# Skipping the padding rows of indirect transfers in a graph-attention and mixture-of-experts kernel

## What is computed

```python
def reference(x, src, dst, ...):
    x = x + gnn(layernorm(x), edge_index, W1, a_src1, a_dst1, b1, W2, a_src2, a_dst2, b2)
    x = x + ffn(layernorm(x), Wg, bg, We, be, W1, b1, W2, b2)

def ffn(xf, ...):                       # G=4 groups, E=8 experts each, D=768, M=384
    ggates, gidx = topk_gates(xf @ Wg + bg, 2)
    egates, eidx = topk_gates(einsum('nd,gde->nge', xf, We) + be, 4)
    combine = gw[:, :, None] * ew
    for g in range(G):
        h = gelu(einsum('nd,edm->enm', xf, W1[g]) + b1[g][:, None, :])
        o = einsum('enm,emd->end', h, W2[g]) + b2[g][:, None, :]
        y = y + einsum('end,ne->nd', o, combine[:, g, :])
```

## Time and profile before

| | |
|---|---|
| median of the runs | 1545.75 us (1545.67 to 1548.69) |
| span of the profiled execution | 1547.4 us |
| PE busy | 1367.3 us, 88% of the span |
| DVE busy | 1158.1 us, 75% |
| ACT busy | 741.6 us, 48% |
| POOL busy | 493.7 us, 32% |
| bytes moved by DMA | 222.06 MB, of them 78.63 MB on the queue that GpSimd issues |
| mixing and routing | about 657 to 816 us of the span |
| expert stage | about 816 us to the end |

### The profile page before, as it was taken

The page is one execution under the profiler, slowest core; times in us unless marked ns, Lnnn a source line. Parts: engine busy times, 40 slices in busy tenths (PEclk is TensorE's granted clock), DMA queues, the critical chain, the costliest instruction groups (busy, mean ns, idle before and its releaser), DMA issues. The chain is left out here.

```text
span 1547.4 us, 30224 instructions
## 1 busy us (share of the span) xinstructions
PE 1367.3 (88%) x7686; PEld 1137.4 (74%) x7687; DVE 1158.1 (75%) x1817; ACT 741.6 (48%) x1175; POOL 493.7 (32%) x554
## 2 busy tenths in 40 slices
PE   6888988878778879799957999999999999999995
PEld 3656656733223339799956899999999999989895
DVE  5479999899999978858886566555565656787782
ACT  3465565255555553412214455444454545665662
POOL 1000000003333410032324445545555545454563
PEclk9999999799999989999977999999999999999998
DMA  4300002041222223144577888877788887999974
GB/s 168 136 10 17 17 14 74 17 176 60 72 93 72 68 59 128 57 124 114 124 206 249 212 231 223 185 182 170 178 210 202 211 203 181 238 282 283 248 163 83
DMA packets 101759, 222.06 MB, mean 144 GB/s; under 512 B 16551, under 2 KB 55719, under 8 KB 101586
## 3 DMA queue, kind: packets, MB, share of 16 engines
q1 hardware_dynamic: 78690, 140.50, 28.3%
q0 software_dynamic: 22240, 78.63, 24.9%
q10 hardware_dynamic: 784, 2.36, 0.4%
HBM read 161.78 MB, written 55.74 MB: 141 GB/s over the span
## 5 line engine op out<-in xcount | busy, mean ns | idle before, releaser
L972 PE MATMUL ps_o<-prob,h_head 128*97 128x512 f32 (+1 forms) x480 | 188.4, 530 | 51.2 <-DVE prob L914 51.2
L2022 POOL DMA_INDIRECT out_nodes<-y,to_index x92 | 153.4, 1667 | 217.4 <-DMA out_nodes<-y,to_index 194.1
L2307 PE MATMUL ps_h<-e_hi,e_xt_hi 128*128 (+1 forms) x546 | 195.7, 359 | 10.4 <-ACT e_xt_hi L2126 6.0
L2292 PE MATMUL ps_y<-e_hi,e_ht_hi 128*128 (+1 forms) x546 | 191.0, 350 | 9.7 <-issue 7.1
L972 PEld LDWEIGHTS ps_o<-prob,h_head 128*97 128x97 f32 x480 | 73.5, 165 | 165.5 <-issue 90.2
L2307 PE MATMUL ps_h<-e_lo,e_xt_hi 128*128 (+1 forms) x546 | 187.3, 343 | 0.0
L2292 PE MATMUL ps_y<-e_hi,e_ht_lo 128*128 (+1 forms) x546 | 183.7, 336 | 0.0
L2292 PE MATMUL ps_y<-e_lo,e_ht_hi 128*128 (+1 forms) x546 | 183.6, 336 | 0.0
L2190 DVE TENSOR_TENSOR e_lo<-raw,e_hi (+1 forms) x189 | 175.6, 953 | 6.2 <-ACT e_hi L2134 5.9
L2143 ACT ACTIVATE y<-ps_y,gate 128x768 f32 (+1 forms) x91 | 82.2, 904 | 170.1 <-PE ps_y L2292 160.4
L2011 POOL DMA_INDIRECT landing<-table,index x93 | 131.3, 1412 | 82.7 <-DVE in_rows L2242 48.1
(11 more groups left out here) (333 smaller groups left out, 3066.0 us busy)
## 6 DMA issues: line engine op xcount, KB each, us to landing
raw<-in_ew SPq DMA_DIRECT2D x192, 384.0 KB
w_room<-rel_dram SPq DMA_DIRECT2D x14, 640.0 KB, 4.7
b_all<-in_eb SPq DMA_DIRECT2D x32, 192.0 KB
al_src<-al_dram SPq DMA_DIRECT2D x1, 5000.0 KB, 14.7
xs<-in_x SPq DMA_DIRECT2D x5, 768.0 KB, 12.8
x_in_t<-in_x SPq DMA_DIRECT2D x10, 384.0 KB, 3.6
out_nodes<-x SPq DMA_DIRECT2D x10, 384.0 KB, 4.1
table<-xf SPq DMA_DIRECT2D x10, 384.0 KB, 2.6
```

The lines of the kernel that those rows point to most:

```text
L972: turn = nc.tensor.matmul(ps_o[u][0:C1 + 1, c, 0:WID[c]], h_head[:, u, t, :], prob[:, t % 2, 512 * c:512 * c + WID[c]], start=(t == 0), st ...
L2022: nc.gpsimd.indirect_dma_start(out, bass.IndirectOffsetOnAxis(to_index[:, w:w + 1], 0), y[:, w, :], None, bounds_check=ROWS - 1, compute_o ...
L2292: last = nc.tensor.matmul(ps_y[:, half, 0:HALF], a, b[:, bass.ds(u, 1), at:at + HALF].rearrange("p o d -> p (o d)"), start=(m == 0), stop= ...
L2307: nc.tensor.matmul(ps_h[:, 0:HID], xt_hi[:, c, :], b[:, bass.ds(e % 2, 1), c * HID:(c + 1) * HID] .rearrange("p o m -> p (o m)"), start=(c ...
```

## The change

Padding keeps its numbers `NP + lane`, but the indirect transfers now have their bound at `NP - 1` and `oob_is_err=False`, so that rows with a larger index are skipped. The 128 extra rows of the table and of the output go, with the two stores that set them to zero and the waits for these. A skipped row of a gather leaves in the landing buffer what was there; so both landing buffers are set to zero once, by two ScalarE copies of a zero tile (the former `pad_rows`, still set by GpSimd) between the last mixing matmul and the first weights, and the first gather waits for these.

```diff
-ROWS = NP + P
...
-        pad_rows = sb("pad_rows", [P, TW])
+        zero_rows = sb("zero_rows", [P, TW])
...
-                sp.wait_ge(filled, 3)
-                sp.dma_start(s.table.ap()[NP:ROWS, :], pad_rows[:, :]).then_inc(pad_out, 16)
-                sp.dma_start(out[NP:ROWS, :], pad_rows[:, 0:D]).then_inc(pad_out, 16)
...
-                sp.wait_ge(pad_out, 32)
...
                     nc.gpsimd.indirect_dma_start(out, bass.IndirectOffsetOnAxis(node_i[:, t:t + 1], 0),
-                                                 bias[:, t % 2, :], None, bounds_check=ROWS - 1,
+                                                 bias[:, t % 2, :], None, bounds_check=NP - 1, oob_is_err=False,
                                                  compute_op=ALU.add).then_inc(added, 16)
...
-                pool.wait_ge(pad_out, 32)
+                pool.wait_ge(landing_set, 2)
                 pool.wait_ge(index_set, 1)
                 nc.gpsimd.indirect_dma_start(s.landing[:, 0, :], None, s.table.ap(),
                                              bass.IndirectOffsetOnAxis(s.index[:, 0:1], 0),
-                                             bounds_check=ROWS - 1).then_inc(s.gathered, 16)
+                                             bounds_check=NP - 1, oob_is_err=False).then_inc(s.gathered, 16)
...
                 act.wait_ge(mixed, NT)
+                act.wait_ge(filled, 3)
+                for u in range(2):
+                    nc.scalar.activation(s.landing[:, u, :], zero_rows[:, :], ACT.Copy).then_inc(landing_set, 1)
                 for piece in range(3):
...
                                                  bass.IndirectOffsetOnAxis(index[:, 0:1], 0),
-                                                 bounds_check=ROWS - 1).then_inc(gathered, 16)
+                                                 bounds_check=NP - 1, oob_is_err=False).then_inc(gathered, 16)
...
                                                  bass.IndirectOffsetOnAxis(to_index[:, w:w + 1], 0),
-                                                 y[:, w, :], None, bounds_check=ROWS - 1,
+                                                 y[:, w, :], None, bounds_check=NP - 1, oob_is_err=False,
                                                  compute_op=ALU.add).then_inc(scattered, 16)
...
-        s.table = nc.dram_tensor("table", [ROWS, TW], F32)
+        s.table = nc.dram_tensor("table", [NP, TW], F32)
...
-    out = nc.dram_tensor("out_nodes", (ROWS, D), F32, kind="ExternalOutput")
+    out = nc.dram_tensor("out_nodes", (NP, D), F32, kind="ExternalOutput")
```

More of the change, by code:

```diff
@@ L1396, in mix_and_route @@
         xf_out = [sem("q_xf_out0"), sem("q_xf_out1")]
-        gates_out, pad_out = sem("q_gates_out"), sem("q_pad_out")
+        gates_out, landing_set = sem("q_gates_out"), sem("q_landing_set")
         consts, filled, casts = sem("f_consts"), sem("q_filled"), sem("f_casts")
@@ L1461, in _ @@
                 nc.gpsimd.memset(br[:, E + G:LOGITS], NOT_A_NEIGHBOUR).then_inc(filled, 1)
-                nc.gpsimd.memset(pad_rows[:, :], 0.0).then_inc(filled, 1)
+                nc.gpsimd.memset(zero_rows[:, :], 0.0).then_inc(filled, 1)
                 nc.gpsimd.memset(half_neg[:, :], -0.5).then_inc(consts, 1)
@@ L2028, in add_bias @@
                     nc.gpsimd.indirect_dma_start(out, bass.IndirectOffsetOnAxis(s.node_i[:, t:t + 1], 0),
-                                                 s.bias[:, t % 2, :], None, bounds_check=ROWS - 1,
+                                                 s.bias[:, t % 2, :], None, bounds_check=NP - 1, oob_is_err=False,
                                                  compute_op=ALU.add).then_inc(added, 16)
```

## The result

| | median of 6 runs, us | profiled execution: span, us |
|---|---|---|
| kernel before | 1546.8 (1545.67 to 1548.77) | 1547.4 |
| changed kernel | 1536.03 (1534.71 to 1542.56) | 1533.0 |

The ratio is 0.992, with a 95% interval of 0.990 to 0.994. The forecast was 1543.8 us with a range from 1537.5, so the gain of 10.8 us lies beyond the range, by 1.5 us at its low end.

A forecast was written before the change was run, and what follows sets the result against it. TensorE was taken as the bound in most of the expert stage, with gains only in its gaps. Terms -1.3 (a) and -0.7 (b), the rest 0, gave -2.0 us: 1545.75 to 1543.75, put at 1543.8, range 1537.5 to 1552.

The forecast's parts named there:

- (b): Skipped rows in each expert's last tile: shorter scatter landings, little reaching TensorE; gain 0.7 us, between 0 and 3.8.
- (a): The all-padding scatter of `k = 0` at the expert stage's start: skipping it gains 1.3 us, between 0 and 1.9.
- my sign of 19.5: Sign for (a): PE busy about 19.5 us or more in the 24 us from the empty `k = 0` scatter on.
- (c): GpSimd's indirect-transfer instructions: cost 0, scatter's median and minimum staying at 1599 and 1592 ns.
- (d): Zeroing the landing buffers on ScalarE before the first weights: two copies of 1.6 us in all, hidden, cost 0.
- (e): Dropped stores of the padding rows on SP: already finished before SP's next DMA was due, gain 0.
- (f): The end: earlier chain savings not felt, only the last landing could shorten, by up to 0.7 us; taken as 0.
- (g): Padding lanes carry earlier rows instead of zeros through all matmuls: no instruction changes shape, products not stored.
- relief comes through: Rival, chance 0.27: shorter scatter chain lets GpSimd be early at most expert changes; -8 us at most, middle 1540.
- the fullest engine: Rival, chance 0.17: landings wait for the DMA engine serving the first lanes, so (b) is 0; 1544.4 us.
- Skipping doesn't cost: Denies the rival, chance 0.18, that lists with skipped rows slow GpSimd's scatter and gather instructions: +8, 1554 us.
- Nothing saved: Rival, chance 0.08: a skipped row still takes a descriptor of the same weight; time stays 1545.75 us.

The follow-up runs named there:

- small weight loads: Kernel before, each of the six weight loads moving only 16 columns from the fourth expert on: 1527.4 us, ratio 0.9863; the same in the changed kernel: 1526.7 us.
- the lanes from 64 on: Kernel before, with only the scatters' padding rows in lanes 64 to 127 skipped: 1543.1 us, ratio 0.9973.
- permuted lanes: Changed kernel with lane order permuted so skipped rows spread evenly over groups of four lanes: 1535.2 and 1535.4 us, ratios 0.9914 and 0.9913.
- the copy: Changed kernel plus a 12 MB table-to-DRAM copy, issued by SyncE behind each expert's weight loads from the fourth expert on: 1551.1 us, ratio 1.0015.

## Why the prediction was wrong

**The step that failed is (b), by its price and by what it left out.** I took 0.7 us, at most 3.8, and nothing for the gathers, because I priced a skipped row by the landing of its own list and the purse by one wait, that before `ps_y`. The runs gave 5.9 us for the scatters and 3.4 for the gathers, each alone. Two things were wrong in this.

*The purse.* The earlier trace rows carry 8.0 us of waits on the path from GpSimd. The small weight loads show 21.5 us: 14.6 us of idle time of PE (22.65 to 8.04) and 6.9 us in its busy time (669.35 to 662.45 us for the same 4323 instructions). I had left out the waits of PE before `ps_xt` and `ps_ht`, those for `e_xt_hi` and those before 860 us, which shrink as well, and the clock. My sentence that the chain touches TensorE by one path alone is wrong by this: PE waited 1.5 us in all for `in_rows` itself in before, and not at all with small loads. Of the 6.9 us of busy time 3.4 are the two drops of the clock in before. The rest may be short pauses that the count of busy time hides: a matmul is shown 0.34 us long and the next one starts after 0.17 us, so up to 0.17 us of each pause counts as busy. The purse could have been had from the windows over the whole stage in one subtraction, 692.0 - 669.35 = 22.65 us of idle time, instead of from two rows of a list of causes.

*The mechanism.* My sum knew skipping as a shorter landing of the skipped list. That part came about as I had it, 18 us of shorter landings where I had 22 for the scatters, and it isn't what decides: gathers alone gain 3.4 us with no scatter list shortened, the lanes from 64 on gain 4.2 us, and 16 us more of shorter landings by permuted lanes give nothing that can be told from zero. The bytes skipped go with the gain in each of these runs, and the gain exists only beside full weight loads. In which landing the other transfers get their room is not shown; it stays open.

**(a) is not confirmed.** The empty scatter does land earlier, in 6.5 and 6.6 us in two profiles of the changed kernel instead of 8.5 in the second of before, and GpSimd's third wait for gates from there on falls from 1.8 to 0.6 us. But the third tile's `y`, for which I had 1.3 us, comes 1.0 us earlier than in before in the first profile of the changed kernel and 1.7 and 1.6 us later in the other two; it is 1.3 us later with scatters alone and with the empty scatter alone. PE busy from 836 to 860 us, 20.59 us in the first profile, met my sign of 19.5 by luck. Counted for 24 us from the empty scatter on, it is in before and then in the three profiles of the changed kernel

```profile
839.60:863.60 24.00, 19.82 (x124) 18.26 (x124) 13.17 (x20) 10.71 (x17) 10.49 (x12) 1.00 1.04 341
```

```profile
837.51:861.51 24.00, 20.83 (x130) 19.26 (x129) 15.24 (x24) 10.93 (x17) 11.90 (x14) 1.00 1.00 324
```

```profile
838.33:862.33 24.00, 19.69 (x114) 18.13 (x113) 14.14 (x22) 9.65 (x15) 11.29 (x13) 0.93 0.99 332
```

```profile
838.62:862.62 24.00, 19.75 (x114) 18.20 (x113) 14.25 (x22) 9.65 (x15) 11.31 (x13) 0.93 0.99 332
```

Before meets the sign as well, and in two of three profiles the clock takes back what the start had gained: the granted clock is 0.93 there. The run with the empty scatter alone, -2.5 us, can't be told from zero.

**(c) was right** in the form that I gave: minimum and median of the scatter's instruction are 1592 and 1600 ns, with no second cluster. But the gather's mean fell from 1412 to 1281 ns, while its median only went from 1070 to 1056: there are fewer of the longer cases. The scatter's mean rose meanwhile, from 1667 to 1704 ns, so less traffic doesn't explain both; what makes these instructions longer wasn't tested. **(d) cost nothing**, as I said, by these rows of ScalarE, and one of VectorE:

```profile
791.61 1.63 ACT L1571 ACTIVATE landing<-zero_rows 128x800 f32<-128x800 f32 x2
793.13 2.30 ACT L1575 ACTIVATE e_hi<-raw 128x768 fp32r<-128x768 f32 x3
795.33 0.23 ACT L1532 ACTIVATE weight<-weight 128x40 f32<-128x40 f32 x1
```

```profile
797.47 0.20 DVE L1664 TENSOR_TENSOR weight<-weight,sel 128x40 f32<-128x40 f32 x1
```

```profile
803.78 1.13 POOL L1518 DMA_INDIRECT landing<-table,index  x1 [0.94 <-POOL index L1512]
```

The two copies took 1.63 us (1.6 foretold), the exponentials ended 1.9 us before VectorE wanted them (1.7 foretold). The gather goes out 12.17 us after ScalarE came to this point. My text counts from the first weights' start, and so measured it is 10.65 us, because the zeroing moved that start; the sign was badly chosen, the cost is 0. **(e) and (f) were right**: the last scatter is issued at 1522.41 us, 6.61 us after the one before, which is the earlier trace rows's 6.60; its tile has 123 real rows. **(g)** no instruction changed its shape.

**The rivals.** The first, that relief comes through, is the nearest: GpSimd is early at more expert changes. It had -8 at most and 0.27, and it should have had the larger chance and a larger end. Its condition, that loaded landings fall too, isn't seen in the full lists (406.0 to 402.1 us in sum), and it had no price for the gathers. The evidence that I held against it, a PE that is 99% busy for most of the stage, is true of the long experts, and of the 12.5 us 1.0 comes before them and 6.6 after the 67th tile. Of the signs, the wait before `ps_y` went from 3.8 to 0.9 us (0.2 and 1.2 in the other two profiles), which I had named as this rival's sign. PE's busy share from 860 to 1300 us rose by 0.7%, within the 1% that I had allowed. The second, the fullest engine, is right for landings and was wrong as a forecast of the time. The Trainium skill, DMA: Bandwidth & Descriptors, section "The descriptor swizzle", gives the first engine partitions 0 to 3 and 32 to 35; the landings agree with it, 4.3 us in the median for fewer than 36 real rows and 5.7 us from 43 on, and 5.1 us for the latter once the real rows are spread. Skipping doesn't cost: the scatter's median and minimum stayed. Nothing saved is excluded by the bytes.

**The range** had its low end at the first rival's end, which came from the earlier trace rows and from the start. With the idle time of the stage as purse it would have been 22 us wide on this side, and the measured 10.8 us would have lain near its middle; that is hindsight, since this purse doesn't say which share of it a change gets.

## What to carry to other kernels

Where the DMA engines are full and a serial chain of landings runs beside the bound engine, don't price bytes only by the landing that they belong to: they also take time from the other transfers. Transfers that are seldom waited for, like these gathers, gave about a third of the gain. Take the purse from the bound engine's idle time over the whole stage, and only then ask the list of waits for the causes. A kernel with its large loads made small, once, gives a bound that no view of the profile shows: what the loads cost by all paths was 21 us here where I had read 8. And take two or three profiles before you read a gain of 1 us at one tile: here its sign changed from one to the next.

## What the runs showed of the hardware

A skipped row of an indirect transfer keeps its packet: 22240 on the queue in both kernels, with 11.9 MB less. In the kernel with scatters alone the trace has 1776 packets of 8 bytes on this queue, one for each skipped row, which take 9 ns each in the median, against 253 ns for a row of 3072 bytes.

TensorE's clock can drop after an idle gap, and then the gap costs twice; but the length of the gap doesn't tell when. Two profiles of the same changed kernel differ by 2.7 us at the third tile. The one that is late, by its timeline (start, us, instruction, idle time before it):

```profile
855.18 0.87 PE L2276 MATMUL ps_xt<-ident,in_rows 128*128 128x128 f32 x6 [1.24 <-DVE in_rows L2240]
857.53 0.56 PE L2290 MATMUL ps_y<-e_hi,e_ht_hi 128*128 x1 [1.48 <-issue]
857.89 0.52 PE L2290 MATMUL ps_y<-e_lo,e_ht_hi 128*128 x1
```

and the other:

```profile
853.19 0.88 PE L2276 MATMUL ps_xt<-ident,in_rows 128*128 128x128 f32 x6 [0.19 <-DVE in_rows L2240]
855.55 0.41 PE L2290 MATMUL ps_y<-e_hi,e_ht_hi 128*128 x1 [1.48 <-issue]
855.80 0.36 PE L2290 MATMUL ps_y<-e_lo,e_ht_hi 128*128 x1
```

After 1.24 and 1.48 us of idle time with six transposes between them, matmuls follow each other at 0.32 us instead of 0.17 to 0.18 until 861 us, the lower of the clock's two levels; the granted clock from 836 to 860 us is 0.95. After 0.19 and 1.48 us it stays at 1.00. Some 11 matmuls at 0.15 us more make 1.6 of the 2.7 us, the gap itself 1.05.

It would be easy to take the first gap for the cause. Two other profiles speak against it. With permuted lanes there is no idle time before `ps_xt`, and the clock drops:

```profile
855.14 0.88 PE L2280 MATMUL ps_xt<-ident,in_rows 128*128 128x128 f32 x6
857.58 0.54 PE L2294 MATMUL ps_y<-e_hi,e_ht_hi 128*128 x1 [1.57 <-issue]
857.92 0.52 PE L2294 MATMUL ps_y<-e_lo,e_ht_hi 128*128 x1
```

With the copy both gaps are there, and it doesn't:

```profile
855.83 0.87 PE L2278 MATMUL ps_xt<-ident,in_rows 128*128 128x128 f32 x6 [1.20 <-DVE in_rows L2242]
858.28 0.41 PE L2292 MATMUL ps_y<-e_hi,e_ht_hi 128*128 x1 [1.57 <-issue]
858.53 0.34 PE L2292 MATMUL ps_y<-e_lo,e_ht_hi 128*128 x1
```

The drop at this place is in five of the nine profiles of kernels with full weight loads that skip the whole empty scatter, unpaced (two of the three of the changed kernel among them), and in none of the five that move it at least in part. That is suggestive, but too few to call it an effect of skipping. In before the same step of 0.32 us begins at 1400.66 us, 0.65 us after a gap of 0.63 us had ended. Why one execution falls and the next doesn't stays open.
